# Causal attention layer on one core: q and k split into two float32r halves instead of three bf16 parts

## What is computed

```python
h = _layernorm(x, axis=-1) * (1 + ca) + sa
q = rope(heads(h @ W_q.T + b_q))            # 16 heads of 16
k = rope(heads(h @ W_k.T + b_k))
v = heads(h @ W_v.T + b_v)
scores = jnp.einsum('bhtd,bhsd->bhts', q, k)
causal = jnp.tril(jnp.ones((t, t), dtype=bool))      # t = 1024
probs = jax.nn.softmax((scores + mask) / jnp.sqrt(jnp.float32(dh)), axis=-1)
out = jnp.einsum('bhts,bhsd->bhtd', probs, v)
```

## Time and profile before

| | |
|---|---|
| median of 3 timed runs | 2565.38 us |
| the three runs | 2565.42, 2529.32, 2565.38 us |
| profiled execution, its own time | 2530.51 us |
| its span in the profile | 2528.8 us |
| busy share of the span | PE 88%, PE weight loads 58%, DVE 66%, ACT 45%, POOL 26% |

### The profile page before, as it was taken

How to read it: one execution, slowest core, us unless ns; L and a number is a source line. 1 busy time by engine, 2 the same in 40 slices (tenths; PEclk the granted TensorE clock), 3 DMA queues, 4 the chain that set the end, 5 groups by cost and what they waited for, 6 DMA issues and landing times. The chain is left out here.

```text
span 2528.8 us, 43948 instructions
## 1 busy us (share of the span) xinstructions
PE 2219.5 (88%) x17528; PEld 1460.1 (58%) x17528; DVE 1679.6 (66%) x2608; ACT 1143.9 (45%) x2530; POOL 646.9 (26%) x609
## 2 busy tenths in 40 slices
PE   4899999999999998399998896999999997389998
PEld 3677777777777777266666453344444433256665
DVE  6655555555555554788886776877777762778885
ACT  0555455555554554233331231466666674233332
POOL 0233333333333332122120234111111114421221
PEclk9999999999999999699998998799999999789999
DMA  6211111111111120200000124433333300100000
GB/s 199 59 35 35 35 35 35 35 35 43 39 35 35 35 51 6 99 1 1 1 1 1 56 82 115 64 51 51 51 51 51 44 2 7 35 5 13 17 15 20
DMA packets 123786, 99.75 MB, mean 39 GB/s; under 512 B 74000, under 2 KB 100496, under 8 KB 123552
## 3 DMA queue, kind: packets, MB, share of 16 engines
q1 hardware_dynamic: 115648, 86.71, 15.1%
q10 hardware_dynamic: 7904, 10.17, 1.3%
q0 software_dynamic: 32, 0.07, 0.0%
HBM read 63.10 MB, written 33.82 MB: 38 GB/s over the span
## 5 line engine op out<-in xcount | busy, mean ns | idle before, releaser
L1630 ACT ACTIVATE PT<-PSUM 128x512 f32<-128x512 f32 (+3 forms) x768 | 332.1, 496 | 203.1 <-PE PSUM L1603 197.9
L1661 DVE TENSOR_REDUCE MXP<-PSUM 128x1 f32<-128x640 f32 (+6 forms) x352 | 349.5, 1026 | 110.1 <-PE PSUM L1564 108.5
L795 POOL TENSOR_TENSOR EX<-EX,RC 128x512 f32<-128x512 f32 x128 | 134.1, 1048 | 418.6 <-DVE RC L727 418.6
L1562 PE MATMUL PSUM<-kS,qS 96*128 96x512 bf16 (+3 forms) x768 | 204.8, 344 | 36.9 <-DMA kS<-k_parts 18.6
L636 ACT ACTIVATE EX<-PSUM,MX 128x128 f32<-128x128 f32 x512 | 147.6, 387 | 170.0 <-DVE MX L718 170.0
L1603 PE MATMUL PSUM<-qS,kS 98*128 98x512 bf16 (+3 forms) x768 | 207.9, 330 | 9.1 <-ACT PT L1630 8.8
L1707 POOL TENSOR_SCALAR_AFFINE_SELECT PT<-PT 128x512 f32<-128x512 f32 x128 | 81.2, 634 | 444.5 <-ACT PT L1630 444.5
L1186 POOL TENSOR_TENSOR FHQ<-FAH,FSH 128x704 f32<-128x704 f32 x64 | 88.2, 1400 | 386.1 <-DVE FAH L829 386.1
L927 PE MATMUL PSUM<-FWU,FXQT 128*128 128x352 f32 x512 | 165.3, 466 | 8.5 <-DVE FHH L1099 8.4
L927 PE MATMUL PSUM<-FWG,FXQT 128*128 128x352 f32 x512 | 167.5, 470 | 5.1 <-ACT FXQT L997 2.7
L1579 PE MATMUL PSUM<-PT,VB 128*32 128x512 f32 (+3 forms) x1536 | 163.6, 498 | 1.4 <-POOL PT L1707 0.6
(11 more groups left out here) (207 smaller groups left out, 4548.8 us busy)
## 6 DMA issues: line engine op xcount, KB each, us to landing
v_rows<-VN SPq DMA_DIRECT2D x64, 256.0 KB, 2.0
V<-v_rows SPq DMA_DIRECT2D x32, 512.0 KB, 5.3
qS<-q_parts SPq DMA_DIRECT2D x96, 128.0 KB, 4.3
kS<-k_parts SPq DMA_DIRECT2D x96, 128.0 KB, 6.7
q_parts<-PARTS SPq DMA_DIRECT2D x16, 384.0 KB, 2.8
k_parts<-PARTS SPq DMA_DIRECT2D x16, 384.0 KB, 2.8
out_x<-X SPq DMA_DIRECT2D x16, 256.0 KB, 2.1
X<-in_x SPq DMA_DIRECT2D x4, 512.0 KB, 8.8
```

The costliest lines, as they stand in the source:

```text
L795: pool.tensor_tensor(EX[:, gr % NEX, :, :], EX[:, gr % NEX, :, :], RC[:, 4 * gr:4 * gr + 4].unsqueeze(2).to_broadcast([128, 4, 128]), ALU. ...
L1562: mm = pe.matmul(ps[:, b, c0:c0 + width], ST["q"][gr % 4][0:96, h, t * 128:(t + 1) * 128], ST["k"][gr % 4][0:96, h, k0:k0 + width], start= ...
L1630: act.activation(PT[at % 2][:, h, 0:N], SB[u % 3][:, 0:N], ACT.Exp, scale=CAUSAL_SCALE).then_inc(s_e, 1)
L1661: dve.tensor_reduce(MXP[:, gr % 2, heads[0]:heads[-1] + 1, t], src, AXX, ALU.max, negate=True).then_inc(s_mx, 1)
```

## The change

q and k are split into two float32r numbers (high by an ACT copy, low by a POOL subtraction), stored as float32. The products are high x high, high x low, low x high: 48 rows of 16. A head with even number sits in partitions 0 to 49, one with odd number in 64 to 113 (48 rows and the two rows of the maxima). h and the weights `WQK`, `WV` are split in the same way, and each projection becomes three float32r matmuls where one float32 matmul was. The mask matmul has the same 64 rows as the head's tile, so it comes in two halves of the contraction. Scores of 256 or 128 columns go two heads to a PSUM bank and exponential. `max_plan` swaps units of single heads toward the other parity, and `LEAD` is 1.45. The loads of q and k, the rows of ones and the reading back of `max_rows` move from SP to POOL. The diff, cut:

```diff
-PART_ROWS = {"q": [0, 1, 2, 0, 1, 0], "k": [0, 0, 0, 1, 1, 2]}
+PRODUCTS = ((0, 0), (0, 1), (1, 0))
+PART_ROWS = {w: [p[n] for p in PRODUCTS] for n, w in enumerate("qk")}
+KP = len(PRODUCTS) * (D // NH)
...
-LEAD = 1.3
+LEAD = 1.45
+def score_units(n):
+    return [[h] for h in range(G)] if width_of(*STEPS[n]) > 256 else [[0, 2], [1, 3]]
...
 # projections, PE
-                pe.wait_ge(g.w_in, 96)
                 turn_x(0)
+                pe.wait_ge(s_wh, 2)
+                pe.wait_ge(s_wl, 2)
...
-                            mm = pe.matmul(ps[:, :], WQK[:, k, c0:c0 + 128], HT[j][:, k, :], start=(k == 0), stop=(k == KT - 1))
+                            for wp, hp in PRODUCTS:
+                                mm = pe.matmul(ps[:, :], WQP[wp][:, k, c0:c0 + 128], HT[j][hp][:, k, :], start=(k == 0 and wp + hp == 0), stop=(k == KT - 1 and wp == 1))
...
 # projections, ACT
+                act.activation(WQP[0][:, :, :], WQK[:, :, :], ACT.Copy).then_inc(s_wh, 1)
+                act.activation(WVP[0][:, :, :], WV[:, :, :], ACT.Copy).then_inc(s_wh, 1)
...
 # projections, DVE
                 normalize(0)
                 dve.memset(g.VAO[:, :, :], 1.0).then_inc(s_one, 1)
+                lows(0)
                 dve.wait_ge(g.w_in, 96)
+                for n, (to, w, hi) in enumerate(((WQP[1], WQK, WQP[0]), (WVP[1], WV, WVP[0]))):
+                    dve.wait_ge(s_wh, n + 1)
+                    dve.tensor_tensor(to[:, :, :], w[:, :, :], hi[:, :, :], ALU.subtract).then_inc(s_wl, 1)
...
-                        if n % 4:
-                            (rest, low)[ab](n - 1)
...
-                        rest(n)
-                        low(n)
+                        if hs + 1 < 2 * NB:
+                            lows(hs + 1)
...
 # projections, POOL
+                def low(n):
+                    pool.wait_ge(s_hi, n + 1)
+                    pool.tensor_tensor(PARTS[:, n % 3, 1, :], RO[:, n % 2, :], PARTS[:, n % 3, 0, :], ALU.subtract).then_inc(s_lo, 1)
...
 # core, max_plan
+                    if gr >= 0 and None not in (this, other) and UNITS[this][0] == UNITS[other][0] >= 4 and this % 2 == 0 and UNITS[this][1][0] % 2 == heads[0] % 2:
+                        stream[at], stream[at + 1] = stream[at + 1], stream[at]
...
 # core, PE
-                            mm = pe.matmul(ps[:, b, c0:c0 + width], ST["q"][gr % 4][0:96, h, t * 128:(t + 1) * 128], ST["k"][gr % 4][0:96, h, k0:k0 + width], start=True, stop=True)
-                            if k0 + width == (t + 1) * 128:
-                                mm = pe.matmul(ps[:, b, c0 + width - 128:c0 + width], IDB[:, :], MU[:, :], start=False, stop=True, skip_group_check=True)
+                            pe.matmul(ps[:, b, c0:c0 + width], part("q", gr, h, KP, slice(t * 128, (t + 1) * 128)), part("k", gr, h, KP, slice(k0, k0 + width)), start=True, stop=True)
+                        for a in range(2):
+                            for b, c0, h, k0, width in places(t, heads):
+                                if k0 + width == (t + 1) * 128:
+                                    sl = slice(64 * (h % 2), 64 * (h % 2) + 64)
+                                    mm = pe.matmul(ps[:, b, c0 + width - 128:c0 + width], IDH[sl, a, :], MUH[sl, a, :], start=False, stop=True, skip_group_check=True)
...
-                pe.wait_ge(s_o, 3)
+                pe.wait_ge(s_o, 128)
...
-                    pe.wait_ge(s_nr, 16 * (gr + 1))
+                    pe.wait_ge(s_nr, 32 * (gr + 1))
...
 # core, POOL
+                for piece in pieces:
+                    load(0, *piece)
+                for n in range(4):
+                    for half in range(2):
+                        pool.dma_start(ST["k"][n][64 * half + KP:64 * half + KP + 2, :, :], A["ones"].rearrange("a (s q) -> a s q", s=2)).then_inc(s_o, 16)
+                for piece in pieces:
+                    load(1, *piece)
...
+                for piece in pieces:
+                    load(2, *piece)
+                max_rows(0)
                 for at in range(GROUPS * NST):
...
                         pool.affine_select(tile, tile, [[0, G], [1, 128]], ALU.is_ge, 0.0, base=0, channel_multiplier=-1).then_inc(s_dg, 1)
+                    if gr + 3 < GROUPS:
+                        if at % NST == 0 and gr:
+                            pool.wait_ge(s_s, gr * NSU)
+                        load(gr + 3, *pieces[at % NST])
...
+                    if at % NST == 9 and gr + 1 < GROUPS:
+                        max_rows(gr + 1)
```

More of the change, by code:

```diff
@@ L8 @@
 i32 = mybir.dt.int32
+f32r = mybir.dt.float32r
 ALU = mybir.AluOpType
@@ L1271, in _ @@
             def _(sp):
-                for n in range(4 * 2 * NB):
+                for n in range(NP):
                     j, w, mt = PIECES[n % 8]
@@ L1426, in places @@
     width = (t + 1) * 128
-    each = 4 if t == 0 else 2 if t == 1 else 1
-    return [(a // each, a % each * width, h, 0, width) for a, h in enumerate(heads)]
+    return [(h % 2, (h - heads[0]) // 2 * width, h, 0, width) for h in heads]
 def max_plan():
@@ L1440, in max_plan @@
     every = G * sum(width_of(j, kt) for j, kt in STEPS)
-    plan, at, cols = {}, 0, 0
+    plan, count, at, cols = {}, {}, 0, 0
     for gr in range(-1, GROUPS):
         for n, (j, kt) in enumerate(STEPS):
-            for h in range(G):
-                if gr < 0 and (n, h) != (NST - 1, G - 1):
+            for i, heads in enumerate(score_units(n)):
+                if gr < 0 and (n, i) != (NST - 1, 1):
                     continue
-                done = gr + 1 if gr < 0 else gr + (sum(G * width_of(*s) for s in STEPS[:n]) + (h + 1) * width_of(j, kt)) / every
-                plan[gr, n, h] = []
+                done = gr + 1 if gr < 0 else gr + (sum(G * width_of(*s) for s in STEPS[:n]) + (i + 1) * len(heads) * width_of(j, kt)) / every
+                plan[gr, n, i] = []
                 while at < len(stream) and cols < whole * (done + LEAD):
-                    plan[gr, n, h].append(stream[at])
+                    this, other = stream[at][1], stream[at + 1][1] if at + 1 < len(stream) else None
+                    if gr >= 0 and None not in (this, other) and UNITS[this][0] == UNITS[other][0] >= 4 and this % 2 == 0 and UNITS[this][1][0] % 2 == heads[0] % 2:
+                        stream[at], stream[at + 1] = stream[at + 1], stream[at]
+                    plan[gr, n, i].append(stream[at])
+                    if stream[at][1] is not None:
+                        count[stream[at]] = len(count) + 1
                     cols += cost[stream[at][1]]
@@ L1453, in max_plan @@
     assert at == len(stream)
-    return plan
+    return plan, count
 def causal_core(g, VA, AO, parts):
     nc, A, IDENT, PSUM = g.nc, g.A, g.IDENT, g.PSUM
-    plan = max_plan()
-    rows = nc.dram_tensor("max_rows", [2, G * T], bf16, kind="Internal").ap()
+    plan, count = max_plan()
+    rows = nc.dram_tensor("max_rows", [2, G * T], f32, kind="Internal").ap()
     with ExitStack() as tmp:
@@ L1484, in causal_core, with exps, part @@
         s_c, s_mx, s_nh, s_nl, s_oa = (g.sem("c_" + n) for n in ("constants", "maxima", "row_high", "row_low", "out_ready"))
-        s_e, s_os, s_o, s_vb, s_dg = (g.sem("c_" + n) for n in ("exp", "out_copied", "ones", "v_ready", "later_keys_cleared"))
+        s_e, s_os, s_vb, s_dg = (g.sem("c_" + n) for n in ("exp", "out_copied", "v_ready", "later_keys_cleared"))
         def diagonals(at):
             return at // NST * 2 * 4 + sum(kt >= 4 * j for j, kt in STEPS[:at % NST])
+        def exps(at):
+            return at // NST * NSU + BEFORE[at % NST + 1]
+        def part(w, gr, h, rows, cols):
+            return ST[w][gr % 4][64 * (h % 2):64 * (h % 2) + rows, h // 2, cols]
         def closes(at):
@@ L1693, in copy_v, with load, max_rows @@
                     pool.tensor_copy(VB[gr % 2][:, :, :, 0:DH + 1], VA[:, gr // NG, :, (gr % NG) * G:(gr % NG + 1) * G, :]).then_inc(s_vb, 1)
-                for n in range(1, 4):
-                    pool.memset(ST["k"][n][96:98, :, :], 1.0).then_inc(s_o, 1)
-                pool.wait_ge(s_o, 3)
+                pieces = [(w, half, at, which) for w in "qk" for half in range(2) for at, which in enumerate(PART_ROWS[w])]
+                def load(gr, w, half, at, which):
+                    row, r = (gr // NG) * D + (gr % NG) * G * DH, 64 * half + DH * at
+                    src = parts[w][row:row + G * DH, :, :].rearrange("(s p r) a t -> p a r s t", s=2, p=2)
+                    pool.dma_start(ST[w][gr % 4][r:r + DH, :, :], src[half, which]).then_inc(s_ld[gr % 4], 16)
+                def max_rows(gr):
+                    pool.wait_ge(s_nw, 16 * (gr + 1))
+                    for half in range(2):
+                        pool.dma_start(ST["q"][gr % 4][64 * half + KP:64 * half + KP + 2, :, :], rows.rearrange("a (s p q) -> p a s q", s=2, p=2)[half]).then_inc(s_nr, 16)
+                for piece in pieces:
+                    load(0, *piece)
+                for n in range(4):
```

(8 more changed lines are left out.)

181 lines of the change are left out of this document (86 added, 95 removed).

## The result

The changed kernel takes 2671.34 us (median of 4 runs, 2667.71 to 2674.36) against 2548.28 before (4 runs on the same chip, 2529.32 to 2565.42): a ratio of 1.050, 95% interval 1.042 to 1.059. It is slower by 5%; the forecast was 2505.

A forecast was written before the change was run, and what follows sets the result against it. PE was taken to bound the projections and steady core, DVE's maxima the core's start. Terms -27 + 6 - 39 = -60 us, off a median of 2565.4, gave 2505 us: own range 2475 to 2530, with rivals 2435 to 2575.

The forecast's parts named there:

- The steady core, -39 us: Core from its first score: groups fall from 31.86 to 29.5 us, so 505 us become 466.
- Columns and pairs: Steady core: paired row halves and fewer columns save 4.05 us per group; pairs missing each other cost 0.4.
- POOL's queue and the rows of the maxima: Steady core: PE waits for maxima rows that POOL issues late, 1.3 us per group; 0.70 us per issue.
- Float32r in the core: Steady core: no cost in the sum; slow float32 weight loads might add 0.5 us per group, 8 in all.
- The projections, -27 us: Projections: three float32r products cut a half sequence from 19.0 to 14.6 us; net saving 27 us, between 10 and 32.
- 0.6 of waiting: Projections: PE's waiting within each half sequence, 0.6 us before, taken as unchanged in the new 14.6 us.
- The 33 us before the late start: Projections: saving over eight half sequences, about 33 us, before PE's later start loses 7.
- The start of the core, +6: Start of the core: POOL's loads and ones 5 us later, LEAD 3.3 more, pairs give 2 back; range 0 to +15.
- two column times for float32r: Rival, projections and core: float32r takes 0.436 us for 512 columns, +203 us, total 2768; chance 0.10.
- Halves do not overlap: Rival, core: row halves run serially, a group takes 33.6 us, the core gains nothing, total about 2568; chance 0.08.
- POOL's DMAs: Rival, core: they cost over 0.70 us or land late, a group takes 31.3 us, total 2534; chance 0.17.
- PE stayed the bound: Against the rival that PE stops being the core's bound, a group falling to 26.5 us, total 2462; chance 0.15.

The follow-up runs named there:

- e16_bf16_halves_64_rows_pool: The changed kernel with q, k and maxima as bf16 halves and all 64 rows of each half named, DMAs still on POOL: 2541.08 us, one run.
- e15_bf16_halves_64_rows: The changed kernel with bf16 halves, loads and maxima's rows back on SP, and all 64 rows of each half named: 2498.95 us, ratio 0.987.
- e17_earlier_turns: The bf16-halves, 64-row kernel with the next half sequence's XN, transposes and low halves one piece earlier in the projections: 2486.33 us, ratio 0.983.
- e7_same_half_neighbours: The changed kernel with heads 0 and 1 in the lower row half and 2 and 3 in the upper: 2715.93 us, one run.

## Why the prediction was wrong, step by step

**The steady core, -39 us, was +121.** The failed step is one that the prediction didn't price: it worked out all columns "at the full clock of 2.4 GHz" and carried that clock over to matmuls of 50 rows. The 1.00 in the earlier trace rows belonged to 96, 98 and 128 rows. In their place the clock stood at half for 23.9 us of a typical group, and naming all 64 rows of each half gave it back. The terms of the sum, now measured one by one, for a typical group:

- Columns and pairs: predicted -4.05 and +0.4. With bf16 halves, all 64 rows and SP's DMAs a group takes 29.7: -2.2. That neighbours in the two halves overlap was right (a pair of 512 in 0.22 us); more of the stream than 0.4 us is lost around it. What takes that 1.5 us was not singled out.
- POOL's queue and the rows of the maxima: predicted +1.3, measured +0.4 for the move. PE's weight loads did wait for these rows, 1.0 us each time in the changed kernel (13.8 us in 14 waits) and 0.5 with bf16 halves (8.1 in 15, `e16_bf16_halves_64_rows_pool`); with SP's DMAs they did not (`e15_bf16_halves_64_rows`). POOL's issue took 0.51 us (twelve loads in 6.1 us), not 0.70.
- Float32r in the core: predicted nothing, with +0.5 beside it by the Trainium skill's rule (TensorE: Matmul & The Clock Gate, Weight-path perf modes). The trace agrees with the rule in kind (184 ns a load against 93), but the cost is 2.3 us, and most of it is in the paired wide matmuls, which the sum beside the rule left out.
- The clock: 40.9 - 32.4 = +8.5 us. Over all fifteen intervals, with those that escape, it is 38.6 - 32.6 = 6.0.

31.9 - 2.2 + 0.4 + 2.3 + 8.5 = 40.9. Without the last two the group would be 30.1, near the 29.5 forecast, in part by luck: 1.5 us too little for the pairs and 0.9 too much for the queue offset each other. The Trainium skill (TensorE: Matmul & The Clock Gate, What's actually happening) describes a gate that is set by how busy PE has been. By that alone a core in which PE is busy for 272 of 280 us should have kept its clock; it had 0.74. Here the measurement decides.

**The projections, -27 us, were -3.** A half sequence took 18.1 us, not 14.6. The price of a float32r matmul was nearly right: 36 in 8.46 us, 0.235 each and not 0.218, +0.8 us in a half sequence; V's 24 took 3.03 and not 2.6, +0.4. The step that failed is "0.6 of waiting": PE waits 2.9 us, +2.3. The prediction compared DVE's total (10 us) with PE's, and not the place of its operations. `lows` takes 3.07 us for two operations, where the two-input subtraction before took 0.69 each. In the changed kernel the same two operations take 1.22 us while POOL is idle and 3.07 beside two of its operations:

```profile
1404.58 1.22 DVE L1379 TENSOR_TENSOR HT<-HF,HT 128x512 fp32r<-128x512 f32 x2
1426.08 3.07 DVE L1379 TENSOR_TENSOR HT<-HF,HT 128x512 fp32r<-128x512 f32 x2 [0.53 <-ACT HT L1350]
```

The Trainium skill (SBUF — State Buffer, SBUF: two separate sides) says that a DVE operation with two inputs in SBUF and a GpSimd operation that reads SBUF exclude each other; the trace agrees with these 3.07 against 1.22 us. POOL is busy for 85 us of this stage where it was 51. `e17_earlier_turns` recovers 2.0 us of each half sequence by order alone. (The 33 us before the late start are 34.5 by the prediction's own figures, 150.8 / 19.0 x 4.35; the net of 27 holds.)

**The start of the core, +6, was +15**, the end of its range. PE's first max score comes 20.7 us after the stage begins (11.8 before; 5 more were predicted), and from there to the first score 39.2 us pass (33.2 before, 1.3 more were predicted). PE ran at half clock in both; what takes the other 5 us of the second stretch was not singled out.

**Rivals.** None was what happened. The one with a time above the forecast's range, two column times for float32r, was wrong in its mechanism: 0.235 us for 512 columns is 1.1 column times. "Halves do not overlap" was wrong as well. POOL's DMAs cost less than forecast, and PE stayed the bound. Even with the clock back in the core only two of the float32r kernel's four runs (2566 to 2614) lie under the range's upper end of 2575.

## What to carry to other kernels

- A clock read from a profile belongs to the shapes that ran then. When a change cuts the rows that matmuls use, price half clock as a rival, and look at the clock in the window of the stage before anything else.
- If rows are left over, fill them with zeros and name them in the instruction: it cost no PE time in the core and gave back 8.5 us in each group of 40.9. The zeros have to be written: their DMAs put off the first max score by 5 us here (1575.3 to 1580.4, float32r), and by 23 where POOL issued them late.
- Put no extra matmuls in to keep the clock up without their price: here they took twice the time expected of them, and the clock fell all the same.
- Pairs in two row halves share one stream and need two weight loads beneath it: bf16 fits (2 x 93 ns under 220), float32r does not (2 x 184).

## What the runs showed of the hardware that I had not expected

- With the same columns and order, scores of 50 and 66 rows ran at a mean clock of 0.66 and 0.81 in the window, 82, 98 and 128 rows at 1.00, and zeros served as well as data.
- With 50 rows in each of two halves the new core loses clock as well: 0.87 in bf16, 0.74 in float32r; with all 64 rows named it has 1.00 in both. The old core with 50 rows in one half has 0.66, but it differs in more than the overlap, and with less overlap (`e7_same_half_neighbours`) the clock was 0.80 and not below 0.74; so that overlap helps the clock is not shown. Why float32r is lower than bf16 there, and why full-array matmuls in between let the clock fall further, stays open.
- The fall is periodic: 23.9 us in each group of 40.9, to within 0.1 us. In the run that started its core 3 us earlier other groups were spared.
